# Two maxima over two elements on VectorE take their constant from an SBUF tile

## The reference, cut to what matters

```
H  = (adj != 0)
w  = first row of adj
Dn = sum_e H[c,e] * w[e];   Dn = where(Dn > 0, 1/Dn, 0)
Be = sum_c H[c,e];          Be = where(Be > 0, 1/Be, 0)
m   = Be[:, None] * (H^T @ (x @ W))
out = Dn[:, None] * (H @ m) + b
```

## Time and profile before

| | |
|---|---|
| median of 3 runs | 1438.51 us (1437.08 to 1438.55) |
| the profiled execution | 1435.79 us, its span 1433.8 us |
| PE (TensorE matmul) busy | 1392.3 us, 97% |
| DVE (VectorE) busy | 1287.9 us, 90%, 4001 instructions |
| ACT (ScalarE) busy | 990.5 us, 69% |
| POOL (GpSimd) busy | 947.7 us, 66%, 1876 instructions |
| mean granted TensorE clock | 0.995 |

### The profile page before, as it was taken

One profiled execution on the slowest core, in us unless ns is written; L12 is line 12 of the kernel. 1 busy time (PEld: TensorE's weight loads), 2 busy tenths in 40 slices (PEclk: granted clock), 3 DMA queues, 4 the chain that ended last, 5 costly groups with the idle time before them and its releaser, 6 DMA issues.

```text
span 1433.8 us, 34585 instructions
## 1 busy us (share of the span) xinstructions
PE 1392.3 (97%) x10900; PEld 1331.7 (93%) x10900; DVE 1287.9 (90%) x4001; ACT 990.5 (69%) x2312; POOL 947.7 (66%) x1876
## 2 busy tenths in 40 slices
PE   3799999999999999999999999999999999999997
PEld 2799999999999999999999999999999999999996
DVE  5789999999999999999999999999999999999984
ACT  3577777777777777777777777777777777777763
POOL 2676676676676676676676676676676676676652
PEclk9999999999999999999999999999999999999999
DMA  7011110120110110110110110110110110110100
GB/s 187 1 42 27 52 51 26 51 51 26 51 51 26 51 51 26 51 51 26 51 51 26 51 51 26 51 51 26 51 51 26 51 51 26 51 51 26 37 19 23
DMA packets 83078, 62.70 MB, mean 44 GB/s; under 512 B 40304, under 2 KB 65520, under 8 KB 83056
## 3 DMA queue, kind: packets, MB, share of 16 engines
q1 hardware_dynamic: 83056, 62.43, 15.8%
HBM read 45.62 MB, written 16.78 MB: 44 GB/s over the span
## 4 chain that ended last, share of the span: by engine, by line
PE 95%; DVE 2%; ACT 1%; issue 0%; DMA 0%; POOL 0%; SPq 0%; DVEq 0%; POOLq 0%
PE BANK L365 29%; PE BANK L330 24%; PE BANK L372 15%; PE WIDE L365 8%; PE WIDE L341 8%; PE WIDE L372 4%; PE BANK L357 2%; PE BANK L315 2%; PE BANK L384 2%; DMA TMP_D<-in_l2wt 0%; PE WIDE L278 0%; DVE BN_B L550 0%; DVE BN_C L550 0%; ACT UHI_D L444 0%; PE WIDE L284 0%
## 5 line engine op out<-in xcount | busy, mean ns | idle before, releaser
L444 ACT ACTIVATE UHI_B<-BANK 128x512 fp32r<-128x512 f32 x96 | 57.0, 593 | 43.9 <-PE BANK L330 43.9
L444 ACT ACTIVATE UHI_D<-BANK 128x512 fp32r<-128x512 f32 x96 | 57.1, 595 | 41.1 <-PE BANK L330 41.1
L444 ACT ACTIVATE UHI_C<-BANK 128x512 fp32r<-128x512 f32 x96 | 57.0, 594 | 41.0 <-PE BANK L330 41.0
L444 ACT ACTIVATE UHI_A<-BANK 128x512 fp32r<-128x512 f32 x96 | 57.1, 594 | 39.1 <-PE BANK L330 39.1
L599 DVE TENSOR_TENSOR ULO_D<-BANK,UHI_D 128x512 fp32r<-128x512 f32 x96 | 65.2, 680 | 18.7 <-ACT UHI_D L444 18.0
L732 POOL TENSOR_TENSOR LN_A<-MV_A,EPS 128x2 f32<-128x2 f32 x80 | 15.9, 198 | 92.3 <-DVE MV_A L558 92.3
L599 DVE TENSOR_TENSOR ULO_A<-BANK,UHI_A 128x512 fp32r<-128x512 f32 x96 | 65.2, 680 | 12.3 <-ACT UHI_A L444 11.8
L599 DVE TENSOR_TENSOR ULO_C<-BANK,UHI_C 128x512 fp32r<-128x512 f32 x96 | 65.1, 678 | 11.1 <-ACT UHI_C L444 9.3
L599 DVE TENSOR_TENSOR ULO_B<-BANK,UHI_B 128x512 fp32r<-128x512 f32 x96 | 65.7, 684 | 10.4 <-ACT UHI_B L444 8.5
L732 POOL TENSOR_TENSOR LN_D<-MV_D,EPS 128x2 f32<-128x2 f32 x80 | 15.8, 197 | 84.7 <-DVE MV_D L558 84.7
L732 POOL TENSOR_TENSOR LN_B<-MV_B,EPS 128x2 f32<-128x2 f32 x80 | 16.7, 209 | 78.2 <-DVE MV_B L558 78.2
(11 more groups left out here) (500 smaller groups left out, 6009.6 us busy)
## 6 DMA issues: line engine op xcount, KB each, us to landing
X_A<-in_xs SPq DMA_DIRECT2D x16, 256.0 KB, 2.8
X_B<-in_xs SPq DMA_DIRECT2D x16, 256.0 KB, 2.8
X_C<-in_xs SPq DMA_DIRECT2D x16, 256.0 KB, 2.8
X_D<-in_xs SPq DMA_DIRECT2D x16, 256.0 KB, 2.8
out_rows<-O_A SPq DMA_DIRECT2D x16, 256.0 KB, 2.0
out_rows<-O_B SPq DMA_DIRECT2D x16, 256.0 KB, 2.1
out_rows<-O_C SPq DMA_DIRECT2D x16, 256.0 KB, 2.1
out_rows<-O_D SPq DMA_DIRECT2D x16, 256.0 KB, 2.1
```

What stands on the lines that cost most here:

```text
L444: nc.scalar.activation(UHI[s][:, 0:J * D], bank(s, step)[:, :], ACT.Copy).then_inc(sem(f"c{step}"), 1)
```

## The change

Two new constant tiles of 128 x 2, ONE (1.0) and LEAST (TINY), are filled by GpSimd at the start. L570 and L579 become a tensor_tensor maximum with these tiles instead of a tensor_scalar maximum with the constant in the instruction. VectorE's first wait is for both signals of ones_ready instead of one.

```diff
-        MONE, MHALF, EIGHTH, EPS = (sb(n, [P, J]) for n in ("MONE", "MHALF", "EIGHTH", "EPS"))
+        MONE, MHALF, EIGHTH, EPS, ONE, LEAST = (sb(n, [P, J]) for n in ("MONE", "MHALF", "EIGHTH", "EPS", "ONE", "LEAST"))
...
-                nc.vector.tensor_scalar(ST[s][:, CNM, :], ST[s][:, CNT, :], 1.0, None, ALU.max).then_inc(sem("cnm"), 1)
+                nc.vector.tensor_tensor(ST[s][:, CNM, :], ST[s][:, CNT, :], ONE[:, :], ALU.max).then_inc(sem("cnm"), 1)
...
-                nc.vector.tensor_scalar(ST[s][:, DNM, :], DNS[s], TINY, None, ALU.max).then_inc(sem("dnm"), 1)
+                nc.vector.tensor_tensor(ST[s][:, DNM, :], DNS[s], LEAST[:, :], ALU.max).then_inc(sem("dnm"), 1)
...
-            dve.wait_ge(sem("ones_ready"), 1)
+            dve.wait_ge(sem("ones_ready"), 2)
...
             nc.gpsimd.memset(EPS[:, :], LN_EPS)
+            nc.gpsimd.memset(ONE[:, :], 1.0)
+            nc.gpsimd.memset(LEAST[:, :], TINY).then_inc(sem("ones_ready"), 1)
```

## The result

The changed kernel takes 1449.69 us (median, 1448.11 to 1450.49) and the kernel before 1437.88 us on the same chip (1437.08 to 1438.55). The ratio is 1.0081, 95% interval 1.0064 to 1.0098: slower by 11.8 us, outside the forecast range. The profiled execution took 1449.24 us. It lies 13.5 us above the profiled one of before (1435.79 us), which was 2.1 us faster than the median.

A forecast was written before the change was run, and what follows sets the result against it. TensorE was taken as the bound, with VectorE holding it 0.15 to 0.2 us at a time. All terms came to 0: 1435.79 + 0 = 1435.8 us profiled, 1438.5 us for the median, range 1431 to 1445.5 us.

The forecast's parts named there:

- (a): L570 and L579 as tensor_tensor, free of GpSimd: -16 to +21 ns each, taken as 0; at worst 2.7 us of VectorE.
- (b): L570 and L579 beside GpSimd's additions: a tensor_tensor would be held as before, L570 some 1.28 us; worth 0.
- (c): Two more GpSimd memsets at the start: 0.1 to 0.2 us, with some 1.7 us of cover; costs nothing.
- The price of the hold: If L570 were not held, all stages would last 21.16 us: 19.7 us saved, 1418.8 us; chance 0.13.
- the last sign named: If L570 stays held and the time moves, look at which streams' L655 is held; no size given.
- The slower rival: Stream A's L655 falls behind GpSimd's L788 after a shorter L579 or L570, 21.16 us stage lengthens: 6.6 us slower, chance 0.08.

The follow-up runs named there:

- the sum form: The kernel before with L570 also writing a running sum to a spare tile allocated last: 1415.22 us against 1435.55; with 64 bytes ahead of UHI_A 1424.42 us.

## Why the prediction was wrong

**The step that failed is a term missing from the sum**, "1435.79 + 0 = 1435.8 us". It had a term for each edited instruction and for the two memsets, and none for where the new tiles stand. The change part by part began with "no instruction is added to VectorE, and none changes its place", as if instructions were all that a diff can move. The missing term measured +12 to +13 us: +13.2 us with the tiles alone, +12.6 with 64 bytes ahead of UHI_A alone, against +11.8 for the whole change. Nothing in the trace of before could have priced it, but the line that adds the tiles is in the diff, in the middle of the list.

**What was right.** (a) The bare cost: unhindered, L570 takes 143 ns and L579 125 ns, 6 to 7 ns less than before, inside the bounds of -16 to +21. (b) The hold does not go away: L570 is held 1.28 us in all four streams, and the two instructions alone are worth 0.05% and -0.04%. (c) The memsets cost nothing: VectorE's first instruction starts at 2.98 us (2.94 before) and is still released by the load of TF_A:

```profile
2.98 0.28 DVE L564 TENSOR_SCALAR_CACHE_REDUCE HT_A<-TF_A 128x128 f32<-128x128 f32 x1 [2.98 <-DMA TF_A<-in_adj_t]
```

The price of the hold, 19.7 us from one short stage against three long ones, measured 20.3 us. One detail was off: L579 of stream D was forecast at 0.15 us and is held at 0.35. It comes with the lost short stage and not from its new form: in the run with the tiles alone it is held at 0.37 us too. And the last sign named, to look at which streams' L655 is held if L570 stays held and the time moves, pointed at half of the answer.

**The slower rival.** Its mechanism took place: L655 of stream A falls behind GpSimd and the short stage is lost. But its trigger was sought in a shorter L570 or L579, and it got 0.08 with the argument that VectorE waits for ScalarE right before L655. The trace after shows how little that protects: VectorE waits the same 0.20 us for ScalarE there and reaches L655 0.08 us later all the same. "The point from which it decides is a shift of about 0.1 us" was read from one round with a lead of 0.07 us; in other rounds of the same trace 0.02 us would do. Its price, 15 x 0.44 = 6.6 us, was too low: the lost stage alone costs 0.60 us a round, 9.0 us over 15. The two effects nearly add up, a round at a time: 0.50 us for the pace and 0.50 to 0.60 for the lost stage, where the changed kernel has 87.00 - 85.95 = 1.05. With 64 bytes ahead of UHI_A, 15 rounds x 0.50 and the 10 held ones x 0.50 make 12.5 us, and 12.6 were measured. In the sum form, where VectorE holds up nobody, the pace alone costs 0.61 us a round (9.2 us over 15), so some 0.1 us of it is hidden where the long stages wait anyway; what hides it is not shown.

## What to carry to other kernels

A new tile in the middle of the allocations moves all tiles behind it, and that may cost or give more than the edit that needs it: allocate new tiles last, and run the tiles without their use as a control before a small difference is put down to instructions. Where TensorE is the bound and its matmuls have the same count but a longer busy time, compare the length of an undisturbed run of the same matmuls before looking for waits. And a short VectorE instruction with a constant that is held beside GpSimd may be free in its running-sum form: here 1.4% of the kernel.

## What the runs showed of the hardware

- The pace of TensorE's 256-column products changes with where the tiles stand, as far as the runs show with the distance in a partition between the weights that stream and the tile that is loaded: 0.45 us against 0.48 us for four in one place, 277 against 284 ns in the mean of one group. Moving all tiles by 64 bytes changes nothing; moving the loaded tiles by 32, 64 or 1984 bytes costs 9 to 13 us of the kernel, by 512, 1024 or 2048 nothing. I take it for a collision of two reads of SBUF, but that is argued only. Why a remainder of 64 is free between 0 and 96 is open, and so is what other remainders do and with how many bytes the pattern repeats. The Trainium skill, "SBUF — State Buffer", section "Who interferes with whom", gives TensorE independent read ports for the moving operand and the loaded one, and has it wait for no other engine; the rows with 64 unused bytes show a pace that hangs on where its two operands stand, and here the measurement decides.
- Two instructions that start within 0.02 us of each other on VectorE and GpSimd settle who is held for 1.1 us. In the changed kernel VectorE's L655 loses with a lag of 0.02 us and then takes 1.55 us, more than the 1.48 us at a lag of 0.10 us. Who wins is not to be read from recorded starts that are equal: with 64 bytes ahead of UHI_A both start at 405.01 and again at 491.44, and VectorE's instruction takes 0.42 us the first time and 1.58 the second. Where GpSimd loses, its addition takes 1.57 us instead of 1.29.
- A tensor_tensor of 2 elements is held by GpSimd's addition just as long as a tensor_scalar of 2 elements: 1.28 us, 9 times its own 0.14 us.
